# Encoder units of a mixture block on one core: expert numbers packed in words, a loop of eight units on TensorE, and q and k projected one unit ahead

## The chip, the core and the metric

The kernel runs on one core of a Trainium2 chip. A core has TensorE (PE; its weight loads are listed as PEld), VectorE (DVE), ScalarE (ACT), GpSimd (POOL) and SyncE (SP), which issues the DMAs. Each engine works through its own list of instructions in order, and semaphores let one engine wait for another. The time is that of one execution on the device, in microseconds (us); the median of several runs is compared. Lower is better.

## What is computed

x has 16 batches of 128 tokens with 256 features. Four steps are each added to it; the change touches the second and the passage to the third.

```python
x = x + L0_xattn(layernorm(x), ctx, ctx, mask)       # attention, one head
# L0_ffn: a mixture of 4 encoder layers, 2 chosen for each batch
gate_logits = x.mean(axis=1) @ gate_w.T + gate_b
_, top_idx = jax.lax.top_k(gate_logits, K)            # K = 2 of E = 4
...
qkv = x @ iw.T + ib                                   # 16 heads of 16
scores = jnp.einsum('bhqd,bhkd->bhqk', q, k) / scale
attn = jax.nn.softmax(scores, axis=-1)
o = jnp.einsum('bhqk,bhkd->bhqd', attn, v) ... @ ow.T + ob
x = _layernorm(x + o, n1w, n1b)
ff = jax.nn.relu(x @ l1w.T + l1b) @ l2w.T + l2b       # 1024 hidden
x = _layernorm(x + ff, n2w, n2b)
...
x = x + L1_xattn(layernorm(x), ctx, ctx)              # causal, 16 heads
x = x + L1_ffn(layernorm(x))                          # shared and chosen experts
```

Only the chosen layers are worked out: 16 batches with 2 each are 32 units. Which weights a unit reads is known only on the device.

## The kernel before

All weights of the four encoder layers lie on chip as two bf16 parts (`w_hi`, `w_lo`). A product is three matmuls (high by high, low by high, high by low; `split_products`, L455 to L462, and the same written out in `projection_qk` and `hidden`). A unit's weights begin at `base = e * W_EXP` with e the expert's number, so their addresses are worked out on TensorE's registers while it runs: one or two register operations for every three matmuls.

The units run as a pipeline over all engines. TensorE's `block(n, ...)` (L720 to L755) does, for unit m = n + 1, the projections of q and k (`projection_qk`, 28 matmuls) and v (`projection_v`, 6), the scores (`scores`), the transpose of the row maxima (`shift_transpose`, L600) and the transposed scores (`scores_T`, L621, 64 small matmuls); for unit n the product with v (`values`, L639), the transposes of its result (`o_rows`, `o_transposes`) and the output projection (`out_proj`); for unit f = n - 1 the transposes of x1 and the first feed-forward product (`hidden`, 56 matmuls in two halves); for unit g = n - 2 the second one (`second`, 24 in two halves). `prep` transposes the normalised tokens of the next batch, every other unit. The numbers of the experts are in `chosen`, one int32 a unit, written by VectorE (L1324, L1332). Lines L453 and L459 to L461 are those of helpers: transposes, and the three matmuls of a product.

Each engine's order within a block is written out by hand: ACT `block` (exps, q and k high parts, copies out of PSUM, relu), VectorE `block` (low parts, maxima, normalisations, sums), POOL `block` (square roots, scales and biases). Blocks -1 to 3 and 28 to 32 stand one after another in the code; blocks 4 to 27 are a loop of two units a turn, twelve turns, on every engine that is concerned. TensorE's loop carries four numbers in registers. It loads the next two in the first of the two blocks, ahead of `shift_transpose`:

```python
_, new = nc.values_load_multi_w_load_instructions(
    chosen[0:1, ds(i * 2 + 2, 2)], engines=engines, min_val=0, max_val=E - 1)
```

Outside of the loop each block begins with a load of one number (`expert`, L716). After the units, `block_c` runs the causal attention and the shared layer in the same manner.

## Time and profile before

| what | value |
|---|---|
| median of 3 runs | 860.49 us (860.32 to 863.5) |
| profiled execution, time | 862.72 us |
| profiled execution, span | 860.7 us |
| TensorE busy | 729.6 us (85%) |
| VectorE busy | 636.4 us (74%) |
| GpSimd busy | 387.1 us (45%) |
| ScalarE busy | 344.0 us (40%) |
| mean granted TensorE clock | 0.91 |

In the profile, "busy" is the time in which an engine works on an instruction. A row of the timeline gives the start, the duration, the engine, the line, the operation, what it writes and reads, the count, and in square brackets how long the engine sat idle before it and who released it; "issue" means that it waited for nothing that the profile shows. Register operations, loads of registers and branches have no rows and are not busy time. A matmul's duration is longer than the distance to the next one's start, because they overlap; the distance is what it costs.

### The profile page before, as it was taken

How to read it: one execution, taken by the hardware profiler on the slowest of the kernel's cores; microseconds unless marked ns; L12 is line 12 of the kernel's file. 1: busy time of each engine (PE TensorE's matmuls, PEld its weight loads, DVE VectorE, ACT ScalarE, POOL GpSimd, SP SyncE). 2: the span in 40 equal slices, each digit the busy share in tenths (PEclk: the TensorE clock that was granted, in tenths of full speed). 3: DMA queues.
4: the chain of work that ended last, by engine and by line, in shares of the span. 5: the costliest groups of instructions: out<-in, count | busy, mean ns of one | idle time of the engine just before them, and what ended most of it. 6: DMA issues, size and time to landing. Idle time of an engine off the chain costs nothing.

```text
span 860.7 us, 29825 instructions
## 1 busy us (share of the span) xinstructions
PE 729.6 (85%) x10940; PEld 580.7 (67%) x10941; DVE 636.4 (74%) x1925; ACT 344.0 (40%) x702; POOL 387.1 (45%) x664
## 2 busy tenths in 40 slices
PE   4688559999999999999999999998988898744885
PEld 3577547877877787878887788885665565422663
DVE  3786655777777777777777777788999999845865
ACT  4554324443434444343434344343454445321210
POOL 2899713344435353444434454443434454335132
PEclk9755578999999999999999999999999999965797
DMA  8877300000000000000000000001222212112000
GB/s 305 271 228 221 105 2 3 3 3 2 0 0 0 0 0 0 0 0 0 0 0 0 0 1 3 9 14 61 85 78 76 85 57 80 55 54 92 14 1 6
DMA packets 24722, 41.21 MB, mean 48 GB/s; under 512 B 3612, under 2 KB 16678, under 8 KB 24408
## 3 DMA queue, kind: packets, MB, share of 16 engines
q1 hardware_dynamic: 23960, 38.70, 13.8%
q0 software_dynamic: 704, 1.71, 0.7%
q8 instruction: 40, 0.66, 0.3%
q14 instruction: 18, 0.15, 0.1%
HBM read 31.88 MB, written 8.91 MB: 47 GB/s over the span
## 4 chain that ended last, share of the span: by engine, by line
PE 71%; DVE 15%; issue 6%; ACT 4%; POOL 2%; DMA 2%; SPq 0%; POOLq 0%; DVEq 0%
PE ps L453 8%; PE ps L459 7%; PE ps L461 6%; PE ps L460 6%; PE ps L639 6%; PE ps L621 5%; DVE mx L1377 4%; PE ps L571 4%; PE ps L677 4%; PE ps L679 3%; PE ps L678 3%; PE ps L573 3%; PE ps L572 3%; PE ps L563 2%; PE ps L675 2%
## 5 line engine op out<-in xcount | busy, mean ns | idle before, releaser
L1783 POOL TENSOR_TENSOR rs<-mv,cst 128x1 f32<-128x1 f32 x132 | 28.9, 219 | 343.3 <-DVE mv L1149 306.2
L1377 DVE TENSOR_REDUCE mx<-ps 128x16 f32<-128x2048 f32 x48 | 109.8, 2287 | 1.6 <-PE ps L594 1.6
L1005 ACT ACTIVATE pT<-ps 128x1024 f32<-128x1024 f32 x96 | 93.0, 1021 | 31.5 <-PE ps L621 29.4
L677 PE MATMUL ps<-xh,w_hi 128*128 128x128 bf16 x512 | 100.1, 220 | 0.0
L679 PE MATMUL ps<-xh,w_lo 128*128 128x128 bf16 x512 | 100.0, 219 | 0.0
L678 PE MATMUL ps<-xl,w_hi 128*128 128x128 bf16 x512 | 99.9, 219 | 0.0
L1785 POOL TENSOR_TENSOR rs<-rs,cst 128x1 f32<-128x1 f32 x132 | 74.2, 562 | 10.3
L459 PE MATMUL ps<-w_hi,hh 128*128 x256 | 70.1, 274 | 0.0
L460 PE MATMUL ps<-w_hi,hl 128*128 x256 | 69.8, 273 | 0.0
L461 PE MATMUL ps<-w_lo,hh 128*128 x256 | 69.8, 273 | 0.0
L1810 POOL TENSOR_TENSOR w_lo<-stage,w_hi 128x384 bf16<-128x384 f32 x64 | 58.8, 945 | 8.3 <-ACT w_hi L927 8.3
L571 PE MATMUL ps<-ycT_hi,w_hi 128*128 128x128 bf16 x256 | 59.6, 233 | 0.0
L572 PE MATMUL ps<-ycT_lo,w_hi 128*128 128x128 bf16 x256 | 57.7, 226 | 0.0
L573 PE MATMUL ps<-ycT_hi,w_lo 128*128 128x128 bf16 x256 | 57.5, 225 | 0.0
L675 PE MATMUL ps<-kst,b1hl 128*128 x256 | 56.1, 219 | 0.0
L927 ACT CAST ooh<-ps 128x256 bf16<-128x256 f32 x48 | 17.9, 372 | 93.3 <-PE ps L453 93.3
L563 PE MATMUL ps<-kst,b1hl 128*128 (+1 forms) x192 | 43.3, 226 | 13.8 <-issue 13.1
L1023 ACT ACTIVATE hh<-ps 128x512 bf16<-128x512 f32 x64 | 38.4, 600 | 38.7 <-PE ps L679 38.7
L677 PEld LDWEIGHTS ps<-xh,w_hi 128*128 x512 | 50.0, 98 | 1.9 <-issue 0.2
L678 PEld LDWEIGHTS ps<-xl,w_hi 128*128 x512 | 50.1, 98 | 0.0
L679 PEld LDWEIGHTS ps<-xh,w_lo 128*128 x512 | 50.0, 98 | 0.1
L600 PE MATMUL ps<-identb,mtile 128*128 128x128 bf16 x48 | 10.9, 227 | 43.2 <-DVE mtile L1385 30.0
(355 smaller groups left out, 2518.1 us busy)
## 6 DMA issues: line engine op xcount, KB each, us to landing
stage<-in_w SPq DMA_DIRECT2D x32, 384.0 KB, 3.9
vec<-in_vec SPq DMA_DIRECT2D x4, 896.0 KB, 5.2
vec<-in_tw SPq DMA_DIRECT2D x12, 256.0 KB, 2.8
ctxc<-in_ctx SPq DMA_DIRECT2D x19, 128.0 KB, 2.1
comb<-x SPq DMA_DIRECT2D x16, 128.0 KB, 1.7
comb<-t SPq DMA_DIRECT2D x16, 128.0 KB, 1.8
shared<-x1b SPq DMA_DIRECT2D x16, 128.0 KB, 1.7
out<-x SPq DMA_DIRECT2D x16, 128.0 KB, 1.8
```

Source lines behind the costliest of these rows:

```text
L459: mm(dst, lhs_hi(j), rhs_hi(j), start=(first and j == 0), stop=False)
L460: mm(dst, lhs_lo(j), rhs_hi(j), start=False, stop=False)
L461: last = mm(dst, lhs_hi(j), rhs_lo(j), start=False, stop=(final and j == chunks - 1))
L571: mm(dst, w1, ycT_hi[:, src, :], start=False, stop=False)
L572: mm(dst, w1, ycT_lo[:, src, :], start=False, stop=False)
L573: last = mm(dst, w2, ycT_hi[:, src, :], start=False, stop=(c == KC - 1))
L677: mm(dst, w(w_hi, c, j), xh[:, c, :], start=False, stop=False)
L678: mm(dst, w(w_hi, c, j), xl[:, c, :], start=False, stop=False)
L679: last = mm(dst, w(w_lo, c, j), xh[:, c, :], start=False, stop=(c == KC - 1))
L1005: A(pT[:, 8 * a:8 * a + 8, :].rearrange("p h q -> p (h q)"), ps[:, 2 * a:2 * a + 2, :].rearrange("p g k -> p (g k)"), ACT.Exp, scale=SCALE ...
L1377: nc.vector.tensor_reduce(mx[:, :], att.rearrange("p g s k -> p (g s) k"), AX.X, ALU.max, negate=True).then_inc(m_max, 1)
L1785: tt(rs[:, i, :], rs[:, i, :], halves, ALU.pow).then_inc(done, 1)
```

## The change

The numbers of eight units are packed into one word: VectorE multiplies each by a power of four, adds them up and writes `words`, four of them, after which it raises `g_words`; TensorE waits for that at the start instead of `g_ready`. TensorE loads one word and takes a digit as `(word >> (2 * k)) & 3`. Its loop now has eight units a turn and three turns, blocks 2 to 25, and loads one word a turn, in the fourth block, behind `second`. The other engines' loops keep two units a turn, from 4 to 27.

Within TensorE's block, q and k are projected for unit n + 2, behind `out_proj` and ahead of `scores_T`; before the first block they are projected once for unit 0. `second` runs its halves in the order 1, 0, the first ahead of `values`; `o_rows` goes behind the second half, `prep` to the place behind `scores`, and `o_transposes` between the halves of `hidden`. VectorE, ACT and POOL get new orders in their blocks to match; `sum2` waits for `l2_xn` of the unit before.

```diff
 
 LOOP_B, LOOP_B_END = 4, 28
+PE_TURN, PE_TURNS = 8, 3
+PE_B, PE_B_END, FETCH = 2, 26, 3
 LOOP_C, LOOP_C_END = 4, 12
...
-C_ID, C_ME, C_MO, C_RNK4, C_ID4, C_RNK8, C_M, C_HALF, C_EPS = 0, 128, 129, 130, 134, 138, 146, 150, 151
-C_ALL = 152
+C_ID, C_ME, C_MO, C_RNK4, C_ID4, C_RNK8, C_M, C_HALF, C_EPS, C_POW = 0, 128, 129, 130, 134, 138, 146, 150, 151, 152
+C_ALL = C_POW + PE_TURN
...
@@ -681,13 +684,15 @@
 
-                pe.wait_ge(hl_b if half else hl_a, u + 1)
+                if half == 1:
+                    pe.wait_ge(hl_b, u + 1)
+                    pe.wait_ge(hl_a, u + 1)
                 j0 = 4 * half
...
                                       lambda j: w_lo[:, ds(base + (W_L2 + (j0 + j) * D), D)],
-                                      4, first=(half == 0), final=(half == 1))
-                if half == 1:
+                                      4, first=(half == 1), final=(half == 0))
+                if half == 0:
                     last.then_inc(ff_psum, 1)
...
-            def expert(u):
-                e = pe.value_load(chosen[0:1, ds(u, 1)], min_val=0, max_val=E - 1)
-                return e * W_EXP, e
-
-            def block(n, slot, ex, km, kp, fetch=None):
+            def block(n, slot, ex, kp, next_k=None, fetch=None):
 
 
                 m, f, g = n + 1, n - 1, n - 2
                 causal_n, causal_m = causal(n), causal(m)
-                base_m, e_m = (None, E) if causal_m else ex(1)
-                projection_qk(km, base_m, e_m)
                 if not isinstance(m, int) or m > 2:
                     pe.wait_ge(hl_b, m - 2)
-                projection_v(base_m)
+                projection_v(None if causal_m else ex(1)[0])
+                if encodes(g):
+                    second(g, 1, ex(-2)[0])
                 if attends(n):
                     values(n, slot, 0)
                     values(n, slot, 1)
-                if encodes(g):
-                    second(g, 0, ex(-2)[0])
-                if attends(n):
-                    o_rows(n)
                 if encodes(f):
                     pe.wait_ge(v_sb, m + 1)
                     x1_transposes(f)
                 if encodes(g):
-                    second(g, 1, ex(-2)[0])
+                    second(g, 0, ex(-2)[0])
+                if fetch is not None:
+                    fetch()
+                if attends(n):
+                    o_rows(n)
                 scores(m, causal_m)
+                if kp is not None:
+                    pe.wait_ge(qk_split, m + 1)
+                    prep(kp, isinstance(kp, int) and kp >= B)
+                if encodes(f):
+                    hidden(f, 1, *ex(-1))
                 if attends(n):
                     o_transposes(n)
                 if encodes(f):
-                    hidden(f, 1, *ex(-1))
                     hidden(f, 0, *ex(-1))
-                if fetch is not None:
-                    fetch()
                 shift_transpose(m)
                 if attends(n):
                     out_proj(n, None if causal_n else ex(0)[0])
-                if kp is not None:
+                if next_k is not None:
                     pe.wait_ge(qk_split, m + 1)
-                    prep(kp, isinstance(kp, int) and kp >= B)
+                    base, e = (None, E) if causal(n + 2) else ex(2)
+                    projection_qk(next_k, base, e)
                 scores_T(m, causal_m)
 
...
-            pe.wait_ge(g_ready, 1)
+            pe.wait_ge(g_words, 1)
...
-            known = {}
-
-            def early(u):
-                if u not in known:
-                    known[u] = expert(u)
-                return known[u]
-            for n in range(-1, LOOP_B):
-                block(n, n % 2, lambda j: early(n + j), batch_of(n + 1), prep_of(n + 2))
-            kept = [nc.alloc_registers(f"expert{i}", engines=engines) for i in range(4)]
-            for i in range(4):
-                nc.regs_mov(kept[i], early(LOOP_B - 2 + i)[1])
-
-            def carried():
-                held = [nc.snap(r, engines=engines, min_val=0, max_val=E - 1) for r in kept]
-                return [(e * W_EXP, e) for e in held]
-            with pe.Fori(LOOP_B // 2, LOOP_B_END // 2) as i:
-                held = carried()
-
-                def fetch():
-                    _, new = nc.values_load_multi_w_load_instructions(
-                        chosen[0:1, ds(i * 2 + 2, 2)], engines=engines, min_val=0, max_val=E - 1)
-                    held.extend((e * W_EXP, e) for e in new)
-                block(i * 2, 0, lambda j: held[2 + j], i, i + 1, fetch)
-                block(i * 2 + 1, 1, lambda j: held[3 + j], i + 1, None)
-                for j in range(4):
-                    nc.regs_mov(kept[j], held[j + 2][1])
-            held = dict(zip(range(LOOP_B_END - 2, LOOP_B_END + 2), carried()))
+            top = 4 ** PE_TURN - 1
+
+            def word_at(k):
+                return nc.values_load_multi_w_load_instructions(words[0:1, ds(k, 1)], engines=engines, min_val=0,
+                                                                max_val=top)[1][0]
+
+            def digit(word, k):
+
+                e = (word >> (2 * k)) & 3
+                return e * W_EXP, e
+            word = word_at(0)
+            projection_qk(0, *digit(word, 0))
+            for n in range(-1, PE_B):
+                block(n, n % 2, lambda j: digit(word, n + j), prep_of(n + 2), batch_of(n + 2))
+            kept = nc.alloc_registers("word", engines=engines)
+            nc.regs_mov(kept, word)
+            with pe.Fori(0, PE_TURNS) as i:
+                held = nc.snap(kept, engines=engines, min_val=0, max_val=top)
+                following = []
+
+                def digit_of(k):
+                    return digit(held, k) if k < PE_TURN else digit(following[0], k - PE_TURN)
+                for t in range(PE_TURN):
+                    n = i * PE_TURN + (PE_B + t)
+                    kp = i * (PE_TURN // 2) + (PE_B + t) // 2 + 1 if t % 2 == 0 else None
+                    next_k = i * (PE_TURN // 2) + (PE_B + t + 2) // 2
+                    block(n, t % 2, lambda j: digit_of(t + 2 + j), kp, next_k,
+                          (lambda: following.append(word_at(i + 1))) if t == FETCH else None)
+                nc.regs_mov(kept, following[0])
+            word = nc.snap(kept, engines=engines, min_val=0, max_val=top)
 
             def late(u):
-                if u not in held:
-                    held[u] = expert(u)
-                return held[u]
-            for n in range(LOOP_B_END, UNITS + 1):
-                if n == UNITS - 1:
+                return digit(word, u - PE_TURN * PE_TURNS)
+            for n in range(PE_B_END, UNITS + 1):
+                if n == UNITS - 2:
                     pe.wait_ge(wc_ready, 1)
-                block(n, n % 2, lambda j: late(n + j), batch_of(n + 1), prep_of(n + 2))
+                block(n, n % 2, lambda j: late(n + j), prep_of(n + 2), batch_of(n + 2) if n < UNITS else None)
...
+                if kp is not None:
+                    prep(kp, 2 * KC if isinstance(kp, int) and kp >= B else KC)
+                if encodes(f):
+                    relu(f, 1)
                 if attends(n):
                     oo(n)
-                if encodes(f):
-                    relu(f, 1)
                 shift(m)
-                if kp is not None:
-                    prep(kp, 2 * KC if isinstance(kp, int) and kp >= B else KC)
                 if encodes(f):
                     relu(f, 0)
@@ -1330,6 +1335,13 @@
             ts(picks[:, :, 1], gs[:, 3, :], -1.0, float(E), ALU.mult, ALU.add).then_inc(g_ready, 1)
+            dve.wait_ge(g_ready, 1)
+            digits = gl[:, 6, 0:UNITS].rearrange("p (g k) -> p g k", k=PE_TURN)
+            g_link(tt(digits, chosen[:, :].rearrange("p (g k) -> p g k", k=PE_TURN),
+                      cst[:, C_POW:C_POW + PE_TURN].rearrange("p (o k) -> p o k", o=1).broadcast_to(
+                          [128, UNITS // PE_TURN, PE_TURN]), ALU.mult))
+            g_link(nc.vector.tensor_reduce(gs[:, 7, 0:UNITS // PE_TURN], digits, AX.X, ALU.add))
+            cp(words[:, :], gs[:, 7, 0:UNITS // PE_TURN]).then_inc(g_words, 1)
...
@@ -1427,6 +1439,8 @@
             def sum2(u, slot):
                 dve.wait_ge(ff_psum, u + 1)
                 dve.wait_ge(x1b_ready, u + 1)
+                if not isinstance(u, int) or u > 0:
+                    dve.wait_ge(l2_xn, u)
                 tt(t2[:, :], ps[:, 7, 0:D], x1b2[slot], ALU.add).then_inc(res2, 1)
...
@@ -1460,43 +1474,41 @@
 
                 m, f, g = n + 1, n - 1, n - 2
                 if encodes(f):
-                    stats1(f)
-                if encodes(g):
-                    h_low(g, 1)
-                    h_low(g, 0)
+                    norm1(f)
+                bias_v(m, 1 - slot, bias_m)
                 if encodes(n - 4):
                     add_expert(n - 4, at(add_b))
+                if kp is not None:
+                    y_of(at(kp[1]), kp[0], UNITS if isinstance(kp[0], int) and kp[0] >= B else kp[0] * 2)
+                qk_low(m)
                 if encodes(f):
-                    norm1(f)
-                bias_v(m, 1 - slot, bias_m)
-                qk_low(m)
-                if ks is not None and kp is None:
-                    y_stats_of(at(ks[1]), ks[0])
+                    x1_low(f)
                 if encodes(n - 3):
                     norm2(n - 3)
+                if encodes(g):
+                    sum2(g, slot)
                 if attends(n):
                     o_norm(n)
-                if encodes(f):
-                    x1_low(f)
-                if encodes(g):
-                    sum2(g, slot)
                 maxima(m)
+                shift_split(m)
                 if attends(n):
                     o_low(n)
-                shift_split(m)
                 if kp is not None:
-                    y_of(at(kp[1]), kp[0], UNITS if isinstance(kp[0], int) and kp[0] >= B else kp[0] * 2)
-                    if ks is not None:
-                        y_stats_of(at(ks[1]), ks[0])
-                if encodes(g):
-                    stats2(g)
+                    y_low(kp[0], 2 * KC if isinstance(kp[0], int) and kp[0] >= B else KC)
+                if encodes(f):
+                    h_low(f, 1)
                 if attends(n):
                     if causal(n):
                         x3(n, n - UNITS, slot)
                     else:
                         sum1(n, slot)
-                if kp is not None:
-                    y_low(kp[0], 2 * KC if isinstance(kp[0], int) and kp[0] >= B else KC)
+                        stats1(n)
+                if encodes(f):
+                    h_low(f, 0)
+                if encodes(g):
+                    stats2(g)
+                if ks is not None:
+                    y_stats_of(at(ks[1]), ks[0])
 
             def stats_c(b):
...
@@ -1875,21 +1884,20 @@
             def block(n, slot, ex, kp, km):
 
                 m, f = n + 1, n - 1
-                if encodes(n - 3):
-                    rstd(2, n - 2, l2_var, l2_veps, l2_rstd)
                 if encodes(f):
                     rstd(1, n, l1_var, l1_veps, l1_rstd)
                 if kp is not None:
                     y_root(kp)
+                if causal(m):
+                    x_bias(m - UNITS, 1 - slot)
+                else:
+                    y_bias(m, km, 1 - slot, ex(1))
                 if encodes(f):
                     affine1(f, ex(-1))
                     x1_bias(f, 1 - slot, ex(-1))
                 if encodes(n - 3):
+                    rstd(2, n - 2, l2_var, l2_veps, l2_rstd)
                     affine2(n - 3, ex(-3))
-                if causal(m):
-                    x_bias(m - UNITS, 1 - slot)
-                else:
-                    y_bias(m, km, 1 - slot, ex(1))
 
```

The order of TensorE's instructions at two places, then VectorE's at one. In the names, `ps` is PSUM, `ooh`/`ool` the high and low part of the attention's result, `ycT_hi`/`ycT_lo` of the tokens, `khm`, `klm`, `qh`, `ql` of k and q, `mT` the transposed maxima; ISA and REGISTER_ALU are register operations. TensorE at the load of numbers in the loop, before:

```order
L679 MATMUL ps<-xh,w_lo 128x128
L831 ISA
L831 TENSOR_LOAD chosen
L831 ISA x4
L600 MATMUL ps<-identb,mtile 128x128 [waits m_split]
L459 ISA [waits oo_split]
```

The same engine, at the load after the change:

```order
L464 MATMUL ps<-w_lo,hh 128x256
L819 ISA
L819 TENSOR_LOAD words
L819 ISA x2
L456 MATMUL ps<-cst,ctxb 128x128 [waits oT_sb]
L456 MATMUL ps<-cst,ctxb 128x128 x3
L597 MATMUL ps<-khm,qh 128x256 [waits qkT_hi]
```

The load moved from behind `hidden` to behind `second`, and has two checks fewer. TensorE from the transposed scores into the next unit of a turn, before:

```order
L621 MATMUL ps<-mT,kst 128x128 x4
L563 ISA [waits y_T_ready]
L563 MATMUL ps<-kst,b1hl 128x128
L571 ISA
L571 MATMUL ps<-ycT_hi,w_hi 128x128
L572 MATMUL ps<-ycT_lo,w_hi 128x128
L573 REGISTER_ALU
```

The same passage after the change:

```order
L624 MATMUL ps<-mT,kst 128x128 x4
L462 ISA [waits hl_b]
L462 MATMUL ps<-w_hi,ycT_hi 128x256
L463 MATMUL ps<-w_hi,ycT_lo 128x256
L464 REGISTER_ALU
L464 MATMUL ps<-w_lo,ycT_hi 128x256
```

Behind the transposed scores now stands v's projection; q's and k's went ahead of them. VectorE around the maxima, in an odd unit of the loop, before:

```order
L1390 RECIPROCAL o_rs<-ps 128x16 [waits o_row]
L1392 TENSOR_TENSOR o<-ps,o_rs 128x256 [waits o_rsum]
L1419 TENSOR_TENSOR xl<-ps,xh 128x256 [waits x1T_hi]
L1430 TENSOR_TENSOR t<-ps,x1b 128x256 [waits x1b_ready,ff_psum]
L1377 TENSOR_REDUCE mx<-ps 128x16 [waits s_psum]
L1397 TENSOR_TENSOR ool<-ps,ooh 128x256 [waits oo_hi]
L1383 CAST mtile<-mx 128x4x16 [waits m_max]
L1385 TENSOR_TENSOR mtile<-mx,mtile 128x4x16 [waits m_hi]
```

The same engine and place after the change:

```order
L1444 TENSOR_TENSOR t<-ps,x1b 128x256 [waits l2_xn,x1b_ready,ff_psum]
L1402 RECIPROCAL o_rs<-ps 128x16 [waits o_row]
L1404 TENSOR_TENSOR o<-ps,o_rs 128x256 [waits o_rsum]
L1389 TENSOR_REDUCE mx<-ps 128x16 [waits s_psum]
L1395 CAST mtile<-mx 128x4x16 [waits m_max]
L1397 TENSOR_TENSOR mtile<-mx,mtile 128x4x16 [waits m_hi]
L1409 TENSOR_TENSOR ool<-ps,ooh 128x256 [waits oo_hi]
```

The low part of the attention's result (`ool`) moved behind the split of the maxima, and the residual sum `t` ahead of the reciprocal.

## Rows read from the trace of the kernel before

**Rows 1.** The page: busy us, share of the span, instructions.

```profile
PE 729.6 (85%) x10940; PEld 580.7 (67%) x10941; DVE 636.4 (74%) x1925; ACT 344.0 (40%) x702; POOL 387.1 (45%) x664
```

**Rows 2.** Stretches: length, busy us (count) by engine, granted clock, DMA share, GB/s.

```profile
202.17:507.71 305.54, 289.52 (x5148) 243.96 (x5149) 226.13 (x640) 130.20 (x254) 134.82 (x242) 1.00 0.00 0
313.43:327.98 14.55, 13.43 (x236) 11.27 (x236) 10.63 (x30) 5.77 (x12) 6.46 (x12) 1.00 0.00 0
...
591.83:712.00 120.17, 102.54 (x1677) 71.41 (x1669) 113.13 (x341) 57.76 (x123) 52.88 (x106) 1.00 0.25 79
```

**Rows 3.** TensorE's waits, 202 to 508 us: total, times, longest.

```profile
PE ps L600 <- issue: 12.1, 11, 1.1
```

**Rows 4.** Timeline of TensorE: q and k, v, the next unit's start.

```profile
300.20 0.23 PE L563 MATMUL ps<-kst,b1hl 128*128 x1
...
302.25 0.28 PE L459 MATMUL ps<-w_hi,ycT_hi 128*128 x1
...
313.43 0.23 PE L563 MATMUL ps<-kst,b1hl 128*128 x1 [0.39 <-issue]
```

**Rows 5.** Timeline of TensorE: q and k with fixed addresses, up to v.

```profile
548.71 0.22 PE L563 MATMUL ps<-kst,b1hl 128*128 128x128 bf16 x1 [0.49 <-DVE ycT_lo L1357]
...
550.27 0.27 PE L459 MATMUL ps<-stage,ycT_hi 128*128 128x256 bf16 x1
```

**Rows 6.** Timeline of TensorE around the load of the turn.

```profile
325.78 0.23 PE L600 MATMUL ps<-identb,mtile 128*128 128x128 bf16 x1 [1.11 <-issue]
...
326.59 0.38 PE L453 MATMUL ps<-cst,y 128*128 128x128 f32 x2
326.90 0.23 PE L621 MATMUL ps<-qh,khm 32*128 32x128 bf16 x4
...
327.98 0.23 PE L563 MATMUL ps<-kst,b1hl 128*128 x1
```

**Rows 7.** Timeline of TensorE: scores, two transposes, hidden, the next unit.

```profile
335.25 0.40 PE L594 MATMUL ps<-khm,qh 32*128 32x256 bf16 x8
335.57 0.44 PE L453 MATMUL ps<-cst,o 128*128 128x128 f32 x2
335.85 0.22 PE L675 MATMUL ps<-kst,b1hl 128*128 x1
...
338.98 0.22 PE L600 MATMUL ps<-identb,mtile 128*128 128x128 bf16 x1
...
341.20 0.23 PE L563 MATMUL ps<-kst,b1hl 128*128 x1 [0.34 <-issue]
```

**Rows 8.** Timeline of VectorE in the same unit.

```profile
333.82 0.26 DVE L1390 RECIPROCAL o_rs<-ps 128x16 f32<-128x16 f32 x1 [0.35 <-PE ps L453]
334.12 0.42 DVE L1392 TENSOR_TENSOR o<-ps,o_rs 128x256 f32<-128x256 f32 x1
...
335.70 2.29 DVE L1377 TENSOR_REDUCE mx<-ps 128x16 f32<-128x2048 f32 x1
337.91 0.41 DVE L1397 TENSOR_TENSOR ool<-ps,ooh 128x256 bf16<-128x256 f32 x1
...
338.46 0.22 DVE L1385 TENSOR_TENSOR mtile<-mx,mtile 128x64 bf16<-128x64 f32 x1
```

**Rows 9.** DMA: all transfers from 220 to 500 us; the page; 500 to 640 us.

```profile
DMA packets 0, 0.00 MB, mean 0 GB/s; under 512 B 0, under 2 KB 0, under 8 KB 0
...
q8 instruction: 40, 0.66, 0.3%
...
q8 instruction: 17, 0.28, 0.9%
```

**Rows 10.** Timeline of TensorE: starts of two units outside of the loop.

```profile
521.25 0.23 PE L563 MATMUL ps<-kst,b1hl 128*128 x1 [0.35 <-issue]
...
534.67 0.23 PE L563 MATMUL ps<-kst,b1hl 128*128 x1 [0.33 <-issue]
```

**Rows 11.** Timeline of VectorE: a product in the choice of experts.

```profile
106.15 0.59 DVE L1329 TENSOR_TENSOR h<-h,cst 128x64 f32<-128x64 f32 x1
```

11 lines of the change are left out of this document (5 added, 6 removed).

## The prediction

> **What bounds the kernel now.** I read the page's busy shares first, then the stretches, TensorE's waits, and its timeline within one turn of the loop. TensorE is 85% busy over the span and VectorE 74% [rows 1]; so I looked for the stretch where TensorE is the fullest. From 202.17 to 507.71 us, where 22 of the 24 units of the loop run, TensorE is busy 289.52 of 305.54 us at granted clock 1.00 and VectorE 226.13 [rows 2]: 305.54/22 = 13.89 us a unit. So TensorE's own stream bounds these units. In this stretch the largest wait of it is 11 idle times before L600, 12.1 us in sum, put down to "issue": it waited for no other engine [rows 3]. From 591.83 us on VectorE is busy 113.13 of 120.17 us [rows 2]: that phase (context attention) has another bound, and its lists hardly change. Whatever is gained must come from the 33 encoder units.
>
> A turn is two units: 300.20 to 313.43 (13.23 us) and on to 327.98 (14.55) [rows 4, 6]. Three losses can be seen in it. (a) The register load of the next two numbers: 1.11 us of idle before L600, once a turn [rows 6]. (b) The back edge: 0.39 us before L563, once a turn [rows 4]. (c) The 28 matmuls of q and k take 302.25 - 300.20 = 2.05 us, although the same 28 with fixed addresses take 550.27 - 548.71 = 1.56 [rows 4, 5]. What differs is the address work on the registers between them. Hidden's 56 matmuls have the same mix of address work and take 338.98 - 335.85 = 3.13 us, the array's pace [rows 7]. I read this so: the instruction side is slower than the array in such code, and the array sees it only when no queued work is left. Hidden starts behind slow transposes; q and k start behind 64 tiny matmuls on row tiles, done in 327.98 - 326.90 = 1.08 us [rows 6], behind which little can pile up.
>
> **The change part by part.** *The unit's length.* Floor: 13.23 less (b) 0.39 less (c) 0.49 = 12.35 us without the transposes of `prep`; they take 326.90 - 326.59 = 0.31 every other unit [rows 6], so 12.50 on average. To this I add four terms.
>
> - v's projection now follows the tiny matmuls: it has 6 matmuls of twice the columns, slower than their address work, so only its first address shows: 0.1.
> - q and k now follow hidden and the output projection. The order shows no pause for the instruction side in between. Hidden's 56 use up an advance of up to 2 x 0.49 = 1 us. The output projection's six matmuls take about 0.65 us (L600 with them 326.59 - 325.78 = 0.81) against 6/28 x 2.05 = 0.44 for the instruction side, and give back 0.2. So I expect 2.05 - 0.2 = 1.85 us, not 1.56: 0.29. The ends are 0 and 0.49; I take a value nearer to the upper one, since hidden spends all but what follows it. So "q and k first" repairs (c) only in part.
> - `o_low` moves behind `shift_split` on VectorE, and the output projection waits for it. From the end of the four transposes VectorE needs 0.2 (release) + 0.26 + 0.42 (o_norm) + 2.21 (maxima, 335.70 to 337.91) + 0.77 (o_low and split, 337.91 to 338.46 + 0.22) = 3.9 us, with a hand-over 4.0 [rows 8]; TensorE needs scores and two transposes 335.85 - 335.25 = 0.60, `prep` 0.15, hidden 3.13 and L600 0.05 = 3.9 [rows 6, 7]. A tie: 0.1 of waiting, between 0 and 0.4. Queued behind that wait are the output projection and q and k; VectorE's sum1 waits for the projection.
> - The eight-unit loop no longer runs from what is loaded. While the two-unit loop runs, the queues move nothing at all from 220 to 500 us, and 17 transfers from 500 to 640 us, where ten units stand one after another in the code [rows 9]. Such a unit costs a little more: 521.25 to 534.67 is 13.42 with a load of 0.33 at its end; less that, 13.09 against 13.22 - 0.34 = 12.88 for the like unit in the loop (327.98 to 341.20) [rows 6, 7, 10]. 0.2 at most; with the terms above partly the same time, I take 0.1.
>
> Sum 12.50 + 0.1 + 0.29 + 0.1 + 0.1 = 13.1 us; against 13.89 that is 0.79 x 24 = 19.0 us gained. That counts (a) and (b) as gone; what stays of them is taken off now.
>
> *Loads.* Twelve become three, one a turn, each of one number. It now stands behind the first half of `second`, so the array has queued work; but hidden then starts with no advance. Between 0.34 (the loads at unit starts, [rows 10]) and 1.11 [rows 6]: 0.7 each, 2.1 us.
>
> *Back edges.* Eleven taken ones become two. If the target is loaded, 0.34 each. If not, the target's code must come first: the queue's 40 transfers fill 0.3% of 16 engines' 860.7 us, 41/40 = 1.0 us each [rows 9]. How long it takes from the branch to the transfer's start no row shows. Between 0.34 and five transfers' time, 5; I take 2.5, two transfers and a half: 5.0 us for two. The Trainium skill ("Runtime: NRT & Kernel Launch", Instruction fetch mechanics) says that TensorE's instruction memory is a FIFO of 128 KiB (2048 instructions) refilled in 16 KiB blocks, that sequential refills are mostly hidden, and that a taken branch to a block outside it stalls for a fetch. The trace agrees in that the two-unit loop moves no code. By its figure a body of eight units (8 x 236 matmuls and as many weight loads, [rows 2]) is far too large to stay, so the skill speaks against this change: every back edge would stall.
>
> *Digits.* The order shows two register operations for each unit's digit in place of the four checks and copies in the loop; the number a unit is the same within two. Nothing.
>
> *Start.* Three more small VectorE steps stand on the chain to the first unit. The like product there takes 0.59 us for 64 columns [rows 11], this one has 32; with the two smaller ones I take 1.0 us lost. Five early loads go (0.34 each, 1.7), and nothing else there is sure: 0.7 gained, rounded up to 1.0 for units 1 to 3, which have the same q and k.
>
> *Units 28 to 31.* The two around 521.25 stand for them, the later one 13.42 us [rows 10]; two go to about 13.1, and in the third the addresses become fixed: 1.7 gained in all, between 0.6 and 2.5.
>
> POOL's new order (y_bias ahead of affine1) delays x1 by 0.7 us; x1's transposes also come later on TensorE, behind both halves of values. If that cover is gone, up to 0.7 us a unit; I take nothing. ACT's `prep` ahead of relu delays relu by one copy; ACT is busy 130.20 of 305.54 us [rows 2]: nothing.
>
> Gain: 19.0 - 2.1 - 5.0 + 1.0 + 1.7 = 14.6 us. The profiled execution took 862.72 us with a span of 860.7, and the median of the runs is 860.49: 862.7 - 14.6 = 848.1 for a profiled one, 860.5 - 14.6 = 845.9 for the median.
>
> **Rivals.** *The array's pace (12.6 us a unit).* If hidden, now split in two by two transposes, lets the instruction side catch up, (c) vanishes, and with it the two terms of 0.1: 28 units x 0.49 = 14 us more, about 832. Against it: hidden and q and k together now need 3 x 0.49 = 1.5 us of advance. *VectorE's chain decides.* exps, qk_hi, qk_low, x1_low, norm2, sum2, o_norm, maxima, split, o_low stand one behind another; if each hand-over costs 0.05 more than I count, the output projection waits 0.4 more: 13.5 us a unit, 28 x 0.4 = 11 more, about 857. For it: the tie above. *The change doesn't do what it says:* the address work of the digits keeps TensorE at 13.9 us, and only loads and edges go: within 3 us of now, 858. *Slower: the code stream.* 24 units from memory are about 2.1 transfers each, 50 transfers. If each holds TensorE for its 1.0 us, that is 50 us less the 2.4 counted: 846 + 48 = 894. It makes the kernel slower from 0.35 us a transfer. Against it: the units that already run like this show 0.1 a transfer.
>
> **How the numbers follow.** Forecast 0.58 (13.1 +- 0.2 us a unit, edges 0.34 to 5: 838 to 854); the array's pace 0.15 (832); VectorE's chain 0.16 (857); no effect 0.06 (858); code stream 0.05 (894). The range from 834 to 857 leaves out half of each of the first two rivals and the last, about 0.2. Half a per cent, 4.3 us, is what a measurement can tell from no change: same is 856 to 865. Of the chain rival half lies below 856. Faster 0.86, same 0.10, slower 0.04. Predicted 846.
>
> **What would show it.** Right: unit starts (first matmul of q and k) about 13.1 us apart; q and k near 1.85 us; two idle times of 2 to 3 us before v's projection, eight units apart; a load idle three times; code transfers throughout the loop. The array's pace shows as q and k in 1.56. The chain rival shows as TensorE waits on ool or mtile in most units, above 0.3 us. The code stream shows as "issue" idle times at irregular places, over 0.4 us each. The forecast fails if the back edge costs over 5 us, or if x1's transposes wait for POOL.

## The result, and the profile after

The changed kernel takes 871.82 us (median of 4 runs, 871.46 to 872.27) against 860.4 us for the kernel before (4 runs): ratio 1.012, 95% interval 1.0104 to 1.0137. The forecast was 845.9 us with a range from 834 to 857, so it was wrong in sign as well as in size. The profiled execution has a span of 869.6 us, 8.9 more than before.

The page of the changed kernel: busy time of the engines, and the queue that moves instructions (transfers, MB, share of 16 engines).

```profile
PE 733.7 (84%) x10940; PEld 579.4 (67%) x10941; DVE 656.0 (75%) x1928; ACT 334.8 (39%) x702; POOL 386.6 (44%) x664
...
q8 instruction: 91, 1.49, 0.7%
```

TensorE is busy for 4.1 us more than before and VectorE for 19.6; 91 transfers of instructions stand where 40 stood [rows 9]. Where did the time go? Three markers cut the span: the first matmul of v's projection at the start and at the end of the 24 units, and the transposed scores of the first unit of the causal attention that has no encoder unit beside it. The changed kernel's first, then those of the kernel before:

```profile
161.58 0.28 PE L462 MATMUL ps<-w_hi,ycT_hi 128*128 x1
...
503.49 0.28 PE L462 MATMUL ps<-w_hi,ycT_hi 128*128 x1
...
584.77 0.23 PE L624 MATMUL ps<-qh,khm 32*128 32x128 bf16 x4
```

```profile
162.25 0.28 PE L459 MATMUL ps<-w_hi,ycT_hi 128*128 x1
...
496.76 0.28 PE L459 MATMUL ps<-w_hi,ycT_hi 128*128 x1
...
576.65 0.23 PE L621 MATMUL ps<-qh,khm 32*128 32x128 bf16 x4
```

| stretch | before | after | change | forecast of the change |
|---|---|---|---|---|
| up to the first marker | 162.25 | 161.58 | -0.7 | -1.0 |
| 24 units | 334.51 | 341.91 | +7.4 | -11.9 (-19.0 + 2.1 + 5.0) |
| units behind them | 79.89 | 81.28 | +1.4 | -1.7 |
| the rest | 284.05 | 284.83 | +0.8 | 0 |

The first and the last stretch say little: in the profiled executions of the kernels below that share the changed kernel's start, the first matmul of q and k begins anywhere from 106.05 to 109.30 us. The stretch of the 24 units is free of that, so each experiment below is read by it too.

TensorE's waits in the changed kernel from 202 to 475 us (sum, times, longest):

```profile
PE ps L462 <- issue: 9.6, 2, 5.0
PE ps L456 <- POOL x L1869: 4.3, 8, 0.6
PE ps L462 <- DVE ool L1409: 1.2, 7, 0.2
```

The 12.1 us before the transpose of the maxima and the 4.1 at the back edges [rows 3, 4] are gone. In their place stand two long pauses, and two kinds of wait that the kernel before did not have.

**The back edges.** TensorE's timeline at the two taken ones, and its windows (length, PE busy, ..., granted clock) from the end of the first pause:

```profile
261.91 0.39 PE L462 MATMUL ps<-w_hi,ycT_hi 128*128 x1 [5.00 <-issue]
...
377.93 0.39 PE L462 MATMUL ps<-w_hi,ycT_hi 128*128 x1 [4.55 <-issue]
```

```profile
261.91:267.00 5.09, 5.09 (x42) 3.64 (x46) 2.29 (x6) 0.00 (x0) 0.25 (x1) 0.50 0.01 3
```

The pause is 5.00 us, and behind it the clock is granted at 0.50, which is 1.2 GHz of the two levels, for the next 5 us; before the pause it was 1.00. v's projection and second take 1.25 + 4.00 us there against 0.67 + 2.71 in other units, 1.9 us more. The DMA view from 256 to 262.5 us, 40 slices of 0.16 us (tenths of the engines' time, all of it instructions):

```profile
DMA  0000070007000000000000000000000000000300
```

Two instruction transfers run at about 256.9 and 257.5 us, each over within a slice of 0.16 us; then the queue is silent until after 262. The pause begins at 256.91, so the transfers are done after 0.7 us of it, and most of the 5 us is not the transfer itself. What the rest is, no view shows.

**The wait for x**, in every other unit. VectorE, GpSimd and TensorE in such a unit:

```profile
318.22 0.18 DVE L1154 BATCH_NORM_AGGREGATE mv<-st 128x2 f32<-128x6 f32 x1
...
320.02 0.41 DVE L1157 TENSOR_SCALAR x<-t,mv,rs 128x256 f32<-128x256 f32 x1 [1.63 <-issue]
```

```profile
317.00 0.55 POOL L1794 TENSOR_TENSOR rs<-rs,cst 128x1 f32<-128x1 f32 x1
...
319.26 0.73 POOL L1857 TENSOR_TENSOR ybo<-y,vec 128x256 f32<-128x256 f32 x1
320.62 0.73 POOL L1867 TENSOR_TENSOR x<-x,vec 128x256 f32<-128x256 f32 x1 [0.63 <-DVE x L1157]
```

```profile
322.39 0.41 PE L456 MATMUL ps<-cst,x 128*128 128x128 f32 x2 [0.47 <-POOL x L1869]
```

The root that norm1 needs is there at 317.55, but norm1 starts at 320.02, after 1.63 us in which VectorE waited for no other engine. In the code its own back edge and its load of two numbers stand there, directly ahead of norm1, because norm1 now opens the turn. In the kernel before this idle time stood ahead of the statistics, behind which nothing hurried (VectorE's waits there, 202 to 507 us):

```profile
DVE st L1146 <- issue: 8.8, 7, 1.3
```

GpSimd's y_bias, the suspect of the prediction, is done at 319.99, before norm1 ends.

**The wait for ool**, in every unit. TensorE and VectorE of the same unit:

```profile
324.48 0.40 PE L597 MATMUL ps<-khm,qh 32*128 32x256 bf16 x8
...
328.44 0.22 PE L603 MATMUL ps<-identb,mtile 128*128 128x128 bf16 x1
328.79 0.28 PE L462 MATMUL ps<-w_hi,ooh 128*128 x1
...
329.47 0.23 PE L566 MATMUL ps<-kst,b1hl 128*128 x1
...
331.65 0.23 PE L624 MATMUL ps<-qh,khm 32*128 32x128 bf16 x4
```

```profile
325.55 2.28 DVE L1389 TENSOR_REDUCE mx<-ps 128x16 f32<-128x2048 f32 x1
...
328.24 0.42 DVE L1409 TENSOR_TENSOR ool<-ps,ooh 128x256 bf16<-128x256 f32 x1
```

The maxima start at 325.55, 0.67 us after the scores end (324.88); before it was 0.05 [rows 7, 8]. ool is ready at 328.66, and the output projection stands 0.35 us behind the transpose instead of 0.06. The output projection then takes 0.68 us here and up to 0.87 in other units, and q and k 331.65 - 329.47 = 2.18, no less than before. The late x is not what makes ool late: in the other unit of the turn x is in time, yet the maxima start at 311.43, 0.43 us behind the scores, and the distance from the transpose to the output projection is 0.39 us. VectorE had waited there 1.29 us for the high part of k from ScalarE, and then had work up to the maxima.

**Slower VectorE instructions.** Three groups of VectorE from 202 to 507 us (count, busy us and mean ns, idle before), of the changed kernel and then of the kernel before:

```profile
L1458 DVE SCALAR_TENSOR_TENSOR x<-y,gate_w,x 128x256 f32 x22 | 15.5, 702 | 0.0
L1157 DVE TENSOR_SCALAR x<-t,mv,rs 128x256 f32<-128x256 f32 x22 | 11.9, 542 | 18.0 <-issue 18.0
...
L1157 DVE TENSOR_SCALAR y<-x,mv,rs 128x256 f32 x11 | 8.4, 768 | 0.0
```

```profile
L1444 DVE SCALAR_TENSOR_TENSOR x<-y,gate_w,x 128x256 f32 x22 | 10.5, 476 | 0.0
L1152 DVE TENSOR_SCALAR x<-t,mv,rs 128x256 f32<-128x256 f32 x22 | 9.0, 408 | 0.0
...
L1152 DVE TENSOR_SCALAR y<-x,mv,rs 128x256 f32 x11 | 4.6, 414 | 1.9 <-issue 1.9
```

The same three instructions of the same size take 226, 134 and 354 ns longer each. One of them (add_expert) in the unit above, while GpSimd multiplies and adds at 320.62 and 321.52, and in the unit before it, where GpSimd is idle for part of the time:

```profile
320.68 0.94 DVE L1458 SCALAR_TENSOR_TENSOR x<-y,gate_w,x 128x256 f32 x1
...
306.71 0.48 DVE L1458 SCALAR_TENSOR_TENSOR x<-y,gate_w,x 128x256 f32 x1
```

The 22 normalisations `x<-t,mv,rs` of the stretch fall into two groups: the 11 that run beside no 128x256 operation of GpSimd all take 0.41 us, and the 11 that share 0.51 to 0.53 us with one take 0.67 to 0.68. The scale `y<-x,mv,rs` takes 0.41 in the two cases without overlap and 0.84 to 0.85 in the nine that overlap by 0.7. In the kernel before none of the three ever runs beside such an operation. The new order puts them side by side. It is 11.7 us of VectorE time in this stretch, nearly 0.9 us of it in the unit shown, ahead of the maxima. So the longer times go with the overlap in every case but the short overlaps of add_expert (0.22 to 0.24 us of overlap, 0.47 to 0.49 us); no run takes the overlap away by itself, and what it costs the whole kernel is not shown.

### The profile page after: what moved, and what is told of

Its sections match the earlier page's. It is cut to its first block, busy times and chain, and to the rows that moved or that the text cites. A ratio compares the mean times of both kernels' runs of the same rounds, so it can differ in the third digit from the quotient of the medians.

```text
span 869.6 us, 29816 instructions
## 1 busy us (share of the span) xinstructions
PE 733.7 (84%) x10940; PEld 579.4 (67%) x10941; DVE 656.0 (75%) x1928; ACT 334.8 (39%) x702; POOL 386.6 (44%) x664
## 4 chain that ended last, share of the span: by engine, by line
PE 41%; DVE 30%; issue 11%; POOL 8%; ACT 7%; DVEq 1%; DMA 1%; POOLq 0%; SPq 0%
DVE mx L1389 10%; PE ps L456 4%; PE ps L462 4%; PE ps L624 4%; PE ps L464 3%; PE ps L463 3%; PE ps L642 3%; PE ps L574 3%; PE ps L576 2%; ACT pT L1010 2%; PE ps L575 2%; DVE y L1157 1%; PE ps L613 1%; PE ps L566 1%; DVE ool L1409 1%
## 5 line engine op out<-in xcount | busy, mean ns | idle before, releaser
L456 PE MATMUL ps<-cst,y 128*128 128x128 f32 x100 | 24.6, 330 | 27.1 <-DVE y L1157 22.2
L1880 POOL TENSOR_TENSOR y<-y,vec 128x256 f32<-128x256 f32 x32 | 23.3, 728 | 50.4 <-DVE y L1157 50.4
```

## The experiments

Unless it says otherwise, an experiment was timed in three rounds. The kernel before had medians of 861.1 to 861.8 us beside them, against 860.4 beside the changed kernel: a difference to its 871.8 us is uncertain by about 1 us. "24 units" is the stretch between the first two markers in the profiled execution.

**1. No back edge on TensorE.** The loop becomes a Python loop, with the words loaded at the same three places:

```diff
-            with pe.Fori(0, PE_TURNS) as i:
-                held = nc.snap(kept, engines=engines, min_val=0, max_val=top)
...
+            for n in range(PE_B, PE_B_END):
+                t, i = (n - PE_B) % PE_TURN, (n - PE_B) // PE_TURN
...
+                block(n, n % 2, lambda j: digit_at(n + j), prep_of(n + 2), batch_of(n + 2),
+                      following if t == FETCH else None)
```

> The changed kernel, with the 24 units of TensorE's loop written out one after another: no back edge on TensorE, the same three loads of words at the same places. Theory A: a back edge to code that is no longer loaded costs 5.0 us of idle time and about 1.9 us at half clock behind it, 6.9 us for each of the two: 871.8 - 13.8 = 858.0 us. Rival B: what was lost lies in the units themselves, and the pauses at the edges only gather it (code that must be fetched anyway): 868 us or more.

857.2 us, ratio to before 0.9953 (0.9939 to 0.9967): 14.6 us less than the changed kernel for two edges. TensorE's waits in the same window keep the other two, and no "issue" line is left:

```profile
PE ps L456 <- POOL x L1864: 5.5, 10, 0.7
PE ps L462 <- DVE ool L1404: 1.6, 10, 0.2
```

The first two markers of this kernel:

```profile
159.58 0.28 PE L462 MATMUL ps<-w_hi,ycT_hi 128*128 x1
...
488.34 0.28 PE L462 MATMUL ps<-w_hi,ycT_hi 128*128 x1
```

The 24 units take 328.76 us in place of 341.91: 13.2 less, 6.6 an edge, where the medians give 7.3. Theory A (6.9) holds.

**2. Four units a turn.** PE_TURN, PE_TURNS = 4, 6 and FETCH = 0, and one more word is loaded behind the loop for the units that follow.

> The changed kernel with four units a turn on TensorE, six turns, so five back edges that are taken instead of two, and six loads of words of four digits. Theory A (each back edge of a body that does not stay loaded costs 6.9 us, whatever its size): three more edges, 871.8 + 20.7 = 892.5 us. Rival C (only what does not fit must be fetched again, and a body of four units, half as long, nearly fits): edges of 0.4 to 2 us, 871.8 - 13.8 + 5 x (0.4 to 2) = 860 to 868 us.

882.1 us, ratio 1.0242 (1.0221 to 1.0262). Against the written-out version that is 24.9 us for five edges, 5.0 each; by the 24 units (353.95 us) 25.2, the same. Neither figure came true: the edge of the shorter body is cheaper than 6.9, but far from 0.4 to 2. One of the five, and the window behind it:

```profile
204.59 0.39 PE L462 MATMUL ps<-w_hi,ycT_hi 128*128 x1 [3.69 <-issue]
```

```profile
204.59:209.00 4.41, 4.41 (x44) 3.22 (x48) 2.29 (x6) 0.00 (x0) 1.42 (x3) 0.61 0.01 4
```

The pause is 3.6 to 3.8 us in place of 4.6 to 5.0, the clock falls again, and in three of five turns the pause also swallows the wait for x. Why a pause is about 1 us longer in the body of eight stays open; experiment 7 has a body of eight as well, without the address work, and pauses of 3.70 and 3.76 us, so the number of units alone is not the reason. That a body of four units is not kept either is shown.

**3. VectorE's turn.** norm1 goes to the end of the turn before:

```diff
+            norm1(LOOP_B - 1)
             with dve.Fori(LOOP_B // 2, LOOP_B_END // 2) as i:
...
-                block(i * 2, 0, bias[0], i - 2, None, (i + 1, i + 1))
+                block(i * 2, 0, bias[0], i - 2, None, (i + 1, i + 1), False)
                 block(i * 2 + 1, 1, bias[1], i - 2, (i + 2, i + 2), None)
+                norm1(i * 2 + 1)
```

> The changed kernel with one step moved on VectorE: the normalisation of x1 (norm1) stands at the end of the turn before, ahead of VectorE's own back edge and load of two numbers, instead of behind them. Theory D: VectorE's start of a turn, an idle time of 1.63 us ahead of norm1, is what makes TensorE wait 0.6 us for x in every other unit: 12 x 0.57 = 6.8 us less, 865.0 us, and no wait on x in the loop. Rival E: GpSimd's y_bias, now ahead of the scale of x1, is what delays it: 871.8 us within 0.5.

865.9 us, 5.9 less than the changed kernel, and the 24 units take 334.33 us, 7.6 less. Theory D said 6.8. The waits of this kernel have no line for x any more:

```profile
PE ps L462 <- issue: 9.4, 2, 4.7
PE ps L462 <- DVE ool L1409: 1.3, 8, 0.2
```

GpSimd's order is untouched and the wait for x is gone, so y_bias ahead of affine1 is not its cause. The wait for ool stays (0.38 and 0.33 us in the mean from the transpose to the output projection in the two units of a turn, 0.37 and 0.34 in the changed kernel), although x is in time.

**4. The kernel before with the load moved.** In the old order nothing but this:

```diff
                 if encodes(g):
                     second(g, 1, ex(-2)[0])
+                if fetch is not None:
+                    fetch()
                 scores(m, causal_m)
...
-                if fetch is not None:
-                    fetch()
                 shift_transpose(m)
```

> The kernel before, with TensorE's load of the next two numbers moved from behind hidden to behind second, nothing else changed. Theory F: the load costs TensorE next to nothing there, because the array has queued work (the changed kernel shows under 0.1 us at its three loads): 12 x 1.0 = 12 us less, 848.5 us. Rival G (the estimate of the prediction, 0.7 us a load wherever it stands, since hidden then starts with no advance): 12 x 0.4 = 5 us less, 855.5 us. Rival H: VectorE or ACT takes the place of the load as what TensorE waits for: 858 us or more, with waits on mtile or ool.

847.04 us, ratio 0.9831 (0.9811 to 0.9851): 14.3 us faster, as much as the whole change was forecast to bring; by the 24 units 334.51 - 321.50 = 13.0. Theory F holds nearly: no idle time is left at the load, but hidden takes 3.42 us in the unit that has it and 3.12 in the other, so a load still costs 0.3 us. The one wait that is left to TensorE is the old back edge:

```profile
PE ps L563 <- issue: 3.5, 10, 0.4
```

**5. The new order in a body that stays loaded.** Two units a turn, two numbers loaded behind second, four carried in registers:

```diff
+            with pe.Fori(PE_B // 2, PE_B_END // 2) as i:
+                held = carried()
...
+                    _, new = nc.values_load_multi_w_load_instructions(
+                        chosen[0:1, ds(i * 2 + 2, 2)], engines=engines, min_val=0, max_val=E - 1)
...
+                block(i * 2, 0, lambda j: held[2 + j], i + 1, i + 1, fetch)
+                block(i * 2 + 1, 1, lambda j: held[3 + j], None, i + 1)
```

> The changed kernel with its order of work as it is, but TensorE's loop as short as before: two units a turn, twelve turns, two numbers loaded a turn behind second and four carried in registers; such a body stayed loaded in the kernel before. Against the written-out version (857.2 us) it has back edges again, but to loaded code. Theory A (an edge costs 0.35 us if its target is loaded; code that comes from memory costs 0.1 us a unit): 857.2 + 12 x 0.35 - 24 x 0.1 = 859.0 us. Rival L (code from memory costs the units 0.3 us or more, which is why they are 0.5 us longer than forecast): 854 us or less. Rival M (the body with q and k ahead does not stay loaded either): 857.2 + 12 x 5 = 917 us.

859.38 us, ratio 0.9968 (0.9936 to 0.9999). No instruction is transferred from 220 to 470 us: this body stays loaded, so rival M falls. The number is that of theory A, but not for its reason. TensorE's waits, and the second unit of a turn from its transposed scores to the next:

```profile
PE ps L456 <- issue: 5.8, 10, 0.6
PE ps L456 <- POOL x L1872: 4.2, 10, 0.5
PE ps L462 <- issue: 3.4, 9, 0.4
PE ps L462 <- DVE ool L1412: 1.6, 10, 0.2
```

```profile
323.72 0.23 PE L624 MATMUL ps<-qh,khm 32*128 32x128 bf16 x4
...
334.68 0.22 PE L566 MATMUL ps<-kst,b1hl 128*128 x1
...
336.69 0.23 PE L624 MATMUL ps<-qh,khm 32*128 32x128 bf16 x4
```

That unit takes 12.97 us, and the like unit of the changed kernel (304.37 to 317.75) 13.38, others of it without a load 13.20 to 13.33. q and k take 2.01 us in place of 2.09 to 2.26. So up to 0.2 to 0.4 us a unit go with code that comes from memory, where the forecast had 0.1; up to, because the numbers of the experts also come from carried registers here and from the digits of a word there, and no run parts the two. Against that gain stand twelve short back edges and a new loss: the load, free in the changed kernel, costs 0.6 us of idle time a turn here. They nearly cancel, so the total alone would have misled.

**6. norm2 out of the chain ahead of the maxima.** With experiment 3, norm2 goes ahead of qk_low, its root ahead of affine1 on GpSimd, and y_bias behind x1_bias.

```diff
+                if encodes(n - 3):
+                    norm2(n - 3)
                 qk_low(m)
                 if encodes(f):
                     x1_low(f)
-                if encodes(n - 3):
-                    norm2(n - 3)
```

> The changed kernel with norm1 at the end of VectorE's turn (as in e3_norm_ahead, 865.9 us), and in addition one step taken out of the stretch between the low parts of q and k and the maxima: norm2 goes ahead of them, into an idle time of 1.3 us, and on GpSimd its root goes ahead of affine1 and y_bias behind x1_bias, so that it is ready there. Theory N: a ring of dependent steps (transposed scores, exps, high and low parts of q and k, maxima, split, ool, output projection, q and k of the unit after the next, transposed scores) bounds the units at 13.3 us; 0.5 us less in it takes the wait for ool (0.2 to 0.3 us a unit) away and lets q and k start with queued work: about 0.3 x 31 = 9 us less, 857 us. Rival O: q and k take 2.17 us because of TensorE's own register work, and the wait for ool only hides the same time: 864 to 866 us.

887.2 us, ratio 1.0285: 21 us slower than experiment 3. Neither theory is tested by it, because the edit made a worse wait: in the first unit of a turn norm2 waits for its root and holds up the low parts of q and k.

```profile
PE ps L456 <- DVE klm L1384: 7.6, 7, 1.1
```

**7. No address work on TensorE.**

```diff
             def digit(word, k):
 
-                e = (word >> (2 * k)) & 3
-                return e * W_EXP, e
+                return 0, 0
```

> The changed kernel with every number of an expert replaced by the constant 0 on TensorE: all units use the weights of the first layer there, the words are still loaded but not decoded, and no address is worked out in registers. Theory P (address work costs TensorE 0.6 us at q and k, 0.15 at the output projection, 0.1 each at second and at the transposes behind it, and these stand in the ring too): 0.9 us a unit less, 31 units, 28 us: 844 us, q and k in 1.56 us. Rival Q: the ring on VectorE and ScalarE holds the units at 13.3 us whatever TensorE does: 866 us, with longer waits for ool.

This kernel leaves the choice of weights out: TensorE reads the first layer's for every unit. 855.5 us, 16.3 less than the changed kernel, not 28. The mechanism of theory P is there: q and k take 1.66 us, and the second unit of a turn 12.54 us against 13.3. But in the first one the wait for x grows from 0.5 or 0.6 to 1.2 or 1.3 us, since TensorE arrives sooner at the same late x. Little more than half of theory P's gain comes through.

```profile
PE ps L456 <- POOL x L1868: 9.7, 8, 1.3
PE ps L462 <- issue: 7.5, 2, 3.8
```

**8. The kernel of experiment 4 with TensorE's loop written out.**

```diff
-            with pe.Fori(LOOP_B // 2, LOOP_B_END // 2) as i:
...
+            for n in range(LOOP_B, LOOP_B_END):
+                block(n, n % 2, lambda j: early(n + j), batch_of(n + 1), prep_of(n + 2),
+                      (lambda n=n: pair_at(n)) if n % 2 == 0 else None)
```

> The kernel before with the load behind second (e6_before_load, 847.0 us), and TensorE's loop of twelve turns written out: the 24 units stand one after another, with the same twelve loads. Theory A: twelve edges of 0.35 us go, and 24 units of code from memory cost 0.1 us each: 847.0 - 4.2 + 2.4 = 845.2 us. Rival R: in this order q and k start without queued work, so every piece of code that comes late costs its whole time: 850 us or more.

847.25 us against 847.04: no difference. Twelve edges of 0.35 us went (4.2 us), so the 24 units from memory cost about as much, 0.17 us each (0.14 by the 24 units, which take 320.71 us against 321.50). Rival R falls.

**9. Experiment 5 with norm1 as in experiment 3.**

> The changed order on a body that stays loaded (e5_turn2, 859.4 us), with norm1 at the end of VectorE's turn (as in e3_norm_ahead). In e5_turn2 the first unit of a turn waits 0.5 us for x, and behind that wait the load, which then finds the array without queued work, costs 0.6. Theory S (the load is free only behind queued work, and the wait for x is what took it away): both shrink, 12 x (0.5 + 0.3) = 9.6 us less, 850 us. Rival T (the load costs 0.6 us in a body with two checked numbers, whatever stands ahead of it): 12 x 0.5 = 6 us less, 853.5 us. Either is slower than the old order with the cheap load (847.0 us), since the wait for ool, 0.3 us a unit, stays.

854.8 us, 4.6 less than experiment 5 (6.3 by the 24 units): the wait for x is gone, but the idle time at the load stays at 0.5 us (theory T).

```profile
PE ps L456 <- issue: 4.8, 10, 0.5
```

**10. The wait for ool taken out of experiment 9.** Two moves:

```diff
                 maxima(m)
-                shift_split(m)
                 if attends(n):
                     o_low(n)
+                shift_split(m)
...
-                shift_transpose(m)
                 if attends(n):
                     out_proj(n, None if causal_n else ex(0)[0])
+                shift_transpose(m)
```

> e10_turn2_norm with the wait for ool taken out: on VectorE o_low ahead of shift_split, as in the kernel before, and on TensorE the output projection ahead of the transpose of the maxima, so that ool is ready 0.4 us earlier and nobody waits for the split ahead of it. Theory U (the wait for ool, 0.25 to 0.3 us in every unit, is what keeps the new order from being faster than the old one): 31 x 0.28 = 8.7 us less than e10_turn2_norm, about 841 us. Rival V (TensorE's next wait stands right behind it: the transposed scores wait for the copy of the transposed maxima, or q and k start with still less queued work and take longer): within 3 us of e10_turn2_norm.

848.1 us, ratio 0.9843 (0.9825 to 0.9862), 6.7 less than experiment 9, between theory U (8.7) and rival V; 4.4 of it lie in the 24 units. In experiment 9 only the second unit of a turn had the wait for ool (0.38 us from the transpose to the output projection), the first, which has the load, did not (0.06). q and k in the second unit of a turn:

```profile
332.16 0.22 PE L566 MATMUL ps<-kst,b1hl 128*128 x1
...
334.01 0.24 PE L624 MATMUL ps<-qh,khm 32*128 32x128 bf16 x4
```

1.85 us, the very number of the prediction; in experiment 9 the same stretch took 2.01. But in the first unit of the same turns q and k take 2.04 us, and in experiment 12, with loaded code and no wait ahead of the output projection either, 2.07 and 2.12. So taking the wait away is not enough to bring 1.85 us, and that one unit in two of one kernel meets the number is in part luck.

**11. The same two moves in the changed kernel itself.**

> The changed kernel as it is (871.8 us, loop of eight units), with only the two moves that take the wait for ool out: o_low ahead of shift_split, and the output projection ahead of the transpose of the maxima. Theory U: 0.3 us in each of 31 units, 9 us less, 862.5 us, with q and k still near 2.1 to 2.2 us. Rival W (the wait also empties TensorE's queue, and without it q and k speed up to 1.85 us as the prediction had it): 0.6 us a unit, 18 us less, 854 us. Rival V (another wait takes its place): 869 us or more.

861.2 us, ratio to the kernel before 1.0 (0.999 to 1.0009): 10.6 us less than the changed kernel, near theory U; by the 24 units (333.70 us) 8.2, 0.34 a unit. q and k stay at 2.11 to 2.26 us (W falls): the wait for ool is not what holds them above 1.85 here. The output projection does go from about 0.8 to 0.66 us.

**12. One word of two digits a turn**, five rounds. In experiment 10 the load becomes as small as the changed kernel's:

```diff
+            g_link(stt(gs[:, 6, :], picks[:, :, 1], 4.0, picks[:, :, 0], ALU.mult, ALU.add))
+            cp(pairs[:, :], gs[:, 6, :]).then_inc(g_words, 1)
...
-                        chosen[0:1, ds(i * 2 + 2, 2)], engines=engines, min_val=0, max_val=E - 1)
-                    held.extend((e * W_EXP, e) for e in new)
+                        pairs[0:1, ds(i + 1, 1)], engines=engines, min_val=0, max_val=15)[1][0]
+                    held.extend(digit(two, k) for k in range(2))
```

> e11_out_first (848.1 us) with the load of each turn made as small as the one of the changed kernel: VectorE also packs the two numbers of each batch into one word behind the words of eight, and TensorE loads one such word a turn and decodes two digits, in place of two numbers with their checks. Theory X (the idle time of 0.6 us behind second, ten times in ten turns of e11_out_first, is the second number and the checks; one word costs at most 0.1, as in the changed kernel): 12 x 0.5 to 0.6 = 6 to 7 us less, 841.5 us, faster than the kernel before by 2.3% and than e6_before_load (847.0 us). Rival Y (the load costs that much in the first unit of any turn, because the array has no queued work there): 848 us within 1.

842.73 us, ratio 0.9779 (0.9763 to 0.9795), the fastest of all. The idle time at the load, 0.57 us in experiment 10, is gone; what is left of TensorE's waits are the back edges:

```profile
PE ps L463 <- issue: 4.3, 10, 0.9
```

Theory X holds for the load. In all it brings 5.4 us in place of 6 to 7 (4.0 by the 24 units, which take 316.16 us against 320.11), because q and k give some back: 2.12 us in the first unit in place of 2.04, and 2.07 in the second in place of 1.85. Why they do is open.

## Why the prediction was wrong

The picture of the kernel before was right: TensorE's stream, with a load, a back edge and the slow address work as its losses. The load was worth what was counted: 12 x 1.11 = 13.3 us, against 14.3 by the medians of experiment 4 and 13.0 by its 24 units. What failed is what the change puts in their place.

- **Back edges**, 5.0 us for two between 0.7 and 10. Experiment 1 gives 14.6 by the medians and 13.2 by the 24 units. The sum took "two transfers and a half" for the pause, at 1.0 us each. That 1.0 us was the time of 16 engines added up: in the trace a transfer is over within a slice of 0.16 us, two are done 0.7 us into the pause, and 4 us of silence follow, whose cause no run shows. And the sum left out the granted clock, which falls to 0.50 behind such a pause: 1.9 us more each. At 8.2 to 9.6 us over its value this is the largest term. The Trainium skill ("Runtime: NRT & Kernel Launch", Instruction fetch mechanics) was cited for exactly this stall; the trace agrees that there is one at every back edge of the loops of eight and four units. The prediction then weighed it with too small a price.
- **x1's cover**, taken at nothing with "up to 0.7 us a unit" named. The cover went in every other unit, 0.6 us each: 5.9 us by the medians of experiment 3, 7.6 by its 24 units. The cause was not GpSimd's y_bias but VectorE's loop. The order of the change shows norm1 moved to the head of VectorE's block; I did not count that VectorE's back edge and load, an idle time of up to 1.3 us a turn that harmed nobody before, stand right ahead of it.
- **The tie at o_low**, 0.1 us with an end at 0.4. It was 0.3: experiment 11 gives 10.6 us over 31 units. The sum let the maxima start right behind the scores; they start 0.67 us behind them in one unit of a turn and 0.43 in the other. Experiment 3 shows that the late x is not the reason. VectorE's longer chain from the high part of k to the maxima, with norm2 and sum2 in it, and the steps slowed beside GpSimd are what the trace offers; which of them decides was not tried. That is the rival "VectorE's chain decides", with a chance of 0.16, at some 0.6 of its price (0.24 of 0.4 us a unit).
- **q and k**, 1.85 us. It was 2.18 in this kernel: 0.33 x 24 = 8 us, in part the same time as the next term. The prediction let queued work carry q and k part of the way from 2.05 to 1.56. With loaded code they take 2.01 to 2.12 us in experiments 5, 9 and 12 and in the first unit of experiment 10, and 1.85 only in its second, so the credit of 0.2 us was not there in general. With fixed addresses (experiment 7) they take 1.66 in the same order: that the address work is what makes them long was right.
- **The code stream**, 0.1 us a unit; up to 0.2 to 0.4 in the new order (experiment 5), 0.17 in the old (experiment 8). The Trainium skill ("Runtime: NRT & Kernel Launch", Instruction fetch mechanics) has sequential refills as mostly hidden; 0.17 us for a unit of about two transfers agrees with that.
- **Loads**, 2.1 us for three. The unit with a load (304.37 to 317.75, 13.38) is hardly longer than its neighbours (13.20 to 13.33), under 0.1 on the upper of them: the load was priced too high, since hidden's lost advance cost nothing here.
- **Start and end.** 0.7 gained for 1.0, which is within what the start differs by from one execution to the next. The units behind the loop lost 1.4 where 1.7 were to be gained: they have the waits for x and for ool too; the first three of them take 40.5 us, and 39.5 in experiment 11.

The terms that failed add up to 9.6 + 5.9 + 0.2 x 31 + 8 = 30 us (by the 24 units 8.2 and 7.6 in place of the first two, the same sum), less 2 for the loads; the miss was 871.8 - 845.9 = 25.9, and v, the transposed scores and the double counting of the code stream gave some back (v's 6 matmuls take 0.67 us against 0.76, where 0.1 was to be lost).

The rival "slower" was put on the code stream within the units, at 0.05. The slowdown came from four places, each 6 to 10 us over its term; the prediction had named every one, as a small cost or as none. Their upper ends (10 us for the edges, 0.7 a unit for x, 0.4 for ool, 0.49 for q and k) would together have given 846 + 5 + 19.6 + 9.3 + 4.8 = 885 us. Each was taken low on its own, and the range did not allow for several going wrong together.

## What to carry to other kernels

Try the smallest part of a change first: moving one load to another place gave 14.3 us, while the whole change lost 11. A longer loop body is a bad trade for a few dear instructions in the loop if the short body stays loaded and the long one does not: make the load cheap and leave the body short, as in the fastest version (842.7 us). When a step moves to the head of an engine's loop body, that engine's branch and register loads come ahead of it, and behind a pause like these, of 3.6 to 5.0 us, the lower clock belongs to its price.

## What the runs showed of the hardware

- A taken branch on TensorE to code that is not loaded: idle for 3.6 to 3.8 us with a body of four units, 4.4 to 5.0 with one of eight, 3.7 to 3.8 with one of eight without address work; 0.34 to 0.39 us if the body of two units stays loaded. Two transfers run in the first 0.7 us of the long pause looked at, none in the 4 us behind them. Behind the two of the changed kernel the granted clock is 0.50 for about 5 us. Per edge in all 5.0 us with four units, 6.6 to 7.3 with eight.
- Code that runs on from memory costs TensorE 0.14 to 0.17 us for a unit of 236 matmuls in the old order, and at most 0.2 to 0.4 in the new one.
- A load of two numbers with their checks on TensorE: 1.11 us of idle time behind hidden [rows 6]; 0.57 behind second in the new order; behind second in the old one no idle time, but hidden is 0.3 us longer. One word, with two checks fewer: no idle time.
- VectorE's back edge with its load of two numbers: 1.63 us idle.
- VectorE's instructions on 128x256 f32 in SBUF alone: 0.41 to 0.48 us by themselves; 0.67 when 0.5 us of it overlap with a 128x256 operation of GpSimd, 0.84 to 0.95 when 0.7 to 0.8 us do. It is read from the traces; no run changes the overlap alone.
